# Attention with both heads of a pair side by side, the V projection spread over it, and the row sums through GpSimd's queue

## What is computed

```
h = layernorm(x) * (1 + ca) + sa                  # sa, ca, ga, ... from silu(c) @ wmod
q, k, v = h @ Wq.T + bq, h @ Wk.T + bk, h @ Wv.T + bv
sim = q @ k.T + bias[bucket(i - j)] * 64**-0.5    # causal mask, no scale on q @ k.T
x = x + ga * (softmax(sim) @ v @ Wo.T + bo)
h = layernorm(x) * (1 + cb) + sb
x = x + gb * (quantize(h) @ ternary(w).T + bias)
```

## Time and profile before

| | us |
|---|---|
| median of 2 runs | 1539.74 (1536.56 to 1542.92) |
| the profiled execution | 1533.55 |
| its slowest core, first to last instruction (core 4) | 1531.6 |
| the other cores | 1494.5 to 1517.7 |
| TensorE matmul busy, core 4 | 1048.7 (68%) |
| VectorE, ScalarE, GpSimd busy | 588.8, 435.2, 119.8 |

### The profile page before, as it was taken

The page is one execution under the profiler, slowest core; times in us unless marked ns, Lnnn a source line. Parts: engine busy times, 40 slices in busy tenths (PEclk is TensorE's granted clock), DMA queues, the critical chain, the costliest instruction groups (busy, mean ns, idle before and its releaser), DMA issues.

```text
span 1531.6 us, 17931 instructions; the slowest of 8 cores (1494.5 to 1531.6 us)
## 1 busy us (share of the span) xinstructions
PE 1048.7 (68%) x3933; PEld 364.3 (24%) x3933; DVE 588.8 (38%) x1412; ACT 435.2 (28%) x784; POOL 119.8 (8%) x230
## 2 busy tenths in 40 slices
PE   0344521499998999989989989989879910011168
PEld 0000200142422422422423423324213300000033
DVE  0061751222412522422323223224325628666667
ACT  0001310045155155154253352451640010222200
POOL 0111221011010110110110110000000000000000
PEclk9555555675855855855756757657858955555579
DMA  8665113410010010110100100000000000000013
GB/s 276 219 220 170 15 15 57 76 13 9 6 11 7 9 12 4 11 12 2 13 10 3 14 8 1 1 2 1 2 2 1 1 28 0 0 0 0 1 69 151
DMA packets 44669, 55.65 MB, mean 36 GB/s; under 512 B 32909, under 2 KB 36317, under 8 KB 41480
## 3 DMA queue, kind: packets, MB, share of 16 engines
q0 software_dynamic: 32352, 33.59, 10.6%
q1 hardware_dynamic: 12216, 20.93, 4.1%
HBM read 52.68 MB, written 10.20 MB: 41 GB/s over the span
## 4 chain that ended last, share of the span: by engine, by line
PE 64%; DVE 16%; DMA 11%; issue 5%; ACT 3%; SPq 1%; DVEq 1%; ACTq 0%; POOLq 0%
PE p_oacc L690 19%; PE p_s L659 17%; PE p_s L615 8%; PE p_s L633 5%; DMA swm<-wm 4%; PE p_s L745 4%; PE p_f L877 4%; DMA sx<-x 2%; PE p_s L585 2%; DMA srowb<-dtaus 2%; DVE shT L416 2%; PE p_mod L374 2%; DVE soT L717 2%; PE p_s L637 1%; DVE stmp L841 1%
## 5 line engine op out<-in xcount | busy, mean ns | idle before, releaser
L669 ACT ACTIVATE sPt<-p_s 128x512 bf16<-128x512 f32 (+3 forms) x640 | 320.7, 535 | 534.0 <-DVE sv L641 281.9
L690 PE MATMUL p_oacc<-sPt,sv 128*65 128x512 bf16 (+3 forms) x640 | 317.1, 550 | 31.1 <-DVE sPt L676 26.0
L659 PE MATMUL p_s<-sqt,skt 64*128 64x512 bf16 (+3 forms) x640 | 301.8, 521 | 8.9 <-DVE soT L591 7.1
L865 PE MATMUL p_tr<-sid,sy 128*128 128x128 bf16 x128 | 25.6, 271 | 203.9 <-DVE sy L861 187.0
L682 DVE TENSOR_TENSOR sPt<-sPt,sE 128x112 bf16<-128x112 bf16 x48 | 10.4, 217 | 339.9 <-ACT sPt L669 339.9
L690 PEld LDWEIGHTS p_oacc<-sPt,sv 128*65 128x65 bf16 x640 | 81.5, 134 | 236.5 <-issue 227.8
L659 PEld LDWEIGHTS p_s<-sqt,skt 64*128 64x128 bf16 x640 | 63.8, 106 | 220.4 <-issue 217.5
L676 DVE TENSOR_TENSOR sPt<-sPt,sE 128x240 bf16<-128x240 bf16 (+1 forms) x256 | 66.0, 268 | 112.3 <-ACT sPt L669 111.7
L633 PE MATMUL p_s<-swv,shT 128*128 128x128 bf16 x1024 | 79.2, 220 | 0.4 <-DVE sv L641 0.4
L374 PE MATMUL p_mod<-swm,scsil 128*1 128x512 f32 x96 | 44.4, 618 | 50.4 <-DMA swm<-wm 49.8
L615 PE MATMUL p_s<-shT,swq 128*128 128x512 bf16 x256 | 72.3, 448 | 7.9 <-DVE sqt L622 5.3
(11 more groups left out here) (104 smaller groups left out, 849.2 us busy)
## 6 DMA issues: line engine op xcount, KB each, us to landing
swm<-wm POOLq DMA_DIRECT2D x24, 1024.0 KB, 5.6
sx<-x SPq DMA_DIRECT2D x16, 512.0 KB
out<-sx SPq DMA_DIRECT2D x16, 512.0 KB
swq<-wq POOLq DMA_DIRECT2D x64, 32.0 KB, 2.1
swk<-wk POOLq DMA_DIRECT2D x64, 32.0 KB, 2.1
swv<-wv POOLq DMA_DIRECT2D x64, 32.0 KB, 2.1
swo<-wo POOLq DMA_DIRECT2D x8, 256.0 KB, 4.0
dtau<-srep SPq DMA_DIRECT2D x16, 96.0 KB
```

Of the source, the lines that this page charges most:

```text
L659: o=o, qc=qc: e.matmul(pb[:, qoff:512], skt[o:o + 64, 128 * kt:128 * (kt + 1)], sqt[o:o + 64, 512 * qc + qoff:512 * (qc + 1)], start=True, ...
L669: sq.add("scalar", lambda e, kt=kt, qoff=qoff, pb=pb: e.activation(sPt[:, kt % 4, qoff:512], pb[:, qoff:512], AF.Exp, bias=EXPB, scale=F1) ...
L690: qc=qc, nkt=nkt: e.matmul(p_oacc[:, 512 * qc + qoff:512 * (qc + 1)], sv[:, kt, 65 * hb:65 * hb + 65], sPt[:, kt % 4, qoff:512], start=(kt ...
L865: sq.add("tensor", lambda e, b=b, c=c, pp=pp: e.transpose(p_tr3[pp][:], sy3[:, b, 128 * c:128 * (c + 1)], sid128[:]), reads=[f"sy:{b}", "s ...
```

## The change

- The two heads of a pair are worked side by side. For each key tile there are two Q K matmuls, one for each half of the array's rows, two exps, two P V matmuls. Q K runs one tile ahead, and `sPt` has two slots for each head.
- `p_oacc` is replaced by two banks, `p_o2[0]` and `p_o2[1]`, used again in every query chunk. The copies to `soT` and of the row sums therefore stand at the end of each chunk.
- The V projection of the next pair is spread in 17 steps (a memset, then 16 groups) over the 40 key-tile steps of this pair's attention, in banks of its own (`p_v`), and `sv` is doubled. The first pair's V projection stays ahead of the attention.
- The row sums are stored in bfloat16, two rows for a pair. `epi_A` reads them back with a load from GpSimd's queue that makes float32 of them; it is written behind chunk 0 of the next pair. `epi_B` has one load that repeats the reciprocals over 64 rows, in place of the four matmuls; it is written behind chunk 1 for head 0 and behind chunk 2 for head 1.

The diff, cut to its core:

```diff
-            sv = sb2("sv", [128, NT, 130], BF16)
-            sPt = sb2("sPt", [128, 4, 512], BF16)
+            sv = sb2("sv", [128, 2, NT, 130], BF16)
+            sPt = sb2("sPt", [128, 2, 2, 512], BF16)
             sE = sb2("sE", [128, NH, 240], BF16)
-            srows1 = sb2("srows1", [1, 4, 512], F32)
-            srs16 = sb2("srs16", [16, 128], F32)
-            srs16b = sb2("srs16b", [16, 128], BF16)
-            srecb4 = sb2("srecb4", [1, 2048], BF16)
-            p_oacc = ps2("p_oacc", [65, SEQ])
+            srowsb = [sb2(f"srowsb{i}", [1, 4, 512], BF16) for i in range(2)]
+            srs32 = sb2("srs32", [32, 128], F32)
+            srs32b = sb2("srs32b", [32, 128], BF16)
+            srbt = sb2("srbt", [128, 2048], BF16)
             p_s = [ps2(f"p_s{i}", [128, 512]) for i in range(4)]
-            sv4 = sv[:].rearrange("p t (g c) -> p t g c", c=65)
+            p_o2 = [ps2(f"p_o2{i}", [65, 512]) for i in range(2)]
+            p_v = [ps2(f"p_v{i}", [128, 128]) for i in range(2)]
+            sv4 = sv[:].rearrange("p b t (g c) -> p b t g c", c=65)
 
...
+                sq.add("gpsimd", lambda e: e.dma_start(
+                    out=srs32[:],
+                    in_=dsumB2[:].rearrange("h (p j) -> (h p) j", p=16)),
+                    reads=["dsB2"], writes=["srs32"], dma=True)
+                sq.add("vector", lambda e: e.reciprocal(srs32[:], srs32[:]),
+                       reads=["srs32"], writes=["srs32"])
+                sq.add("vector", lambda e: e.tensor_copy(srs32b[:], srs32[:]),
+                       reads=["srs32"], writes=["srs32b"])
                 sq.add("sync", lambda e: e.dma_start(
-                    out=srs16[:],
-                    in_=dsum[:].rearrange("o (p j) -> (o p) j", p=16)),
-                    reads=["dsum"], writes=["srs16"], dma=True)
-                sq.add("vector", lambda e: e.reciprocal(srs16[:], srs16[:]),
-                       reads=["srs16"], writes=["srs16"])
-                sq.add("vector", lambda e: e.tensor_copy(srs16b[:], srs16[:]),
-                       reads=["srs16"], writes=["srs16b"])
-                sq.add("sync", lambda e: e.dma_start(
-                    out=dsumb[:].rearrange("o (p j) -> (o p) j", p=16),
-                    in_=srs16b[:]),
-                    reads=["srs16b"], writes=["dsumb"], dma=True)
-                sq.add("sync", lambda e: e.dma_start(
-                    out=srecb4[:], in_=dsumb[:]),
-                    reads=["dsumb"], writes=["srecb4"], dma=True)
-
-            def epi_B(d0, o0):
+                    out=dsumB3[:].rearrange("h (p j) -> (h p) j", p=16),
+                    in_=srs32b[:]),
+                    reads=["srs32b"], writes=["dsB3"], dma=True)
+
+            def epi_B(d0, hb0):
+                o0 = 64 * hb0
+                src = AP(dsumB3, 2048 * hb0, [[0, 64], [1, 2048]])
+                sq.add("sync", lambda e, src=src, o=o0: e.dma_start(
+                    out=srbt[o:o + 64, :], in_=src),
+                    reads=["dsB3"], writes=[f"srbt:{hb0}"], dma=True)
                 for qc in range(NQC):
-                    pb = p_s[qc % 4]
-                    pt = f"ps:{qc % 4}"
-                    sq.add("tensor", lambda e, qc=qc, pb=pb: e.matmul(
-                        pb[0:64, :], ones1[:, 0:64],
-                        srecb4[0:1, 512 * qc:512 * (qc + 1)],
-                        start=True, stop=True),
-                        reads=["srecb4"], writes=[pt])
-                    sq.add("vector", lambda e, qc=qc, o=o0, d=d0, pb=pb,
-                           pt=pt: e.tensor_mul(
+                    sq.add("vector", lambda e, qc=qc, o=o0, d=d0: e.tensor_mul(
                         soT[o:o + 64, d, 512 * qc:512 * (qc + 1)],
                         soT[o:o + 64, d, 512 * qc:512 * (qc + 1)],
-                        pb[0:64, :]),
-                        reads=[pt, "soT"], writes=["soT"])
-
-            epi = {"a": None, "b": None}
+                        srbt[o:o + 64, 512 * qc:512 * (qc + 1)]),
+                        reads=[f"srbt:{hb0}", "soT"], writes=["soT"])
 
...
+            def vproj_steps(d):
...
+                def memset_ones(vb=vb):
+                    sq.add("vector", lambda e, vb=vb: e.memset(
+                        sv4[:, vb, :, :, 64:65], 1.0),
+                        writes=[f"svones:{vb}"])
+                steps.append(memset_ones)
                 for t in range(NT):
+                    def grp(t=t, wb=wb, vb=vb, d=d):
+                        pv = p_v[t % 2]
+                        pvt = f"pv:{t % 2}"
+                        for c in range(NCH):
+                            sq.add("tensor", lambda e, wb=wb, c=c, t=t,
+                                   pv=pv: e.matmul(
+                                pv[:],
+                                shT[:, c, 128 * t:128 * (t + 1)],
+                                swv[:, wb, c, :], start=(c == 0), stop=False),
+                                reads=[f"wv:{wb}", f"hT:{c}:{t // 4}"],
+                                writes=[pvt])
+                        sq.add("tensor", lambda e, d=d, pv=pv: e.matmul(
+                            pv[:], ones1[:],
+                            sbvb[:, 128 * d:128 * (d + 1)],
+                            start=False, stop=True),
+                            reads=["bvb", "ones1"], writes=[pvt])
+                        sq.add("vector", lambda e, t=t, vb=vb, pv=pv: e.tensor_copy(
+                            sv4[:, vb, t, :, 0:64],
+                            pv[:].rearrange("p (g c) -> p g c", c=64)),
+                            reads=[pvt], writes=[f"sv:{vb}:{t}"])
...
+            prev = None
+            for d in range(NP):
+                vb = d % 2
+                qkproj(d)
+                if d == 0:
+                    for st in vproj_steps(0):
+                        st()
                 if d + 2 < NP:
                     wload(d + 2)
+                vsteps = vproj_steps(d + 1) if d + 1 < NP else []
+                vinj = [0]
+                step_idx = [0]
+                TOT = sum(4 * qc + 4 for qc in range(NQC))
...
+                    def emit_pv(hb, kt, qc=qc, nkt=nkt, vb=vb):
+                        qoff = max(0, 128 * kt - 512 * qc)
+                        sl = kt % 2
+                        sq.add("tensor", lambda e, kt=kt, qoff=qoff, hb=hb,
+                               sl=sl, nkt=nkt, vb=vb: e.matmul(
+                                   p_o2[hb][:, qoff:512],
+                                   sv[:, vb, kt, 65 * hb:65 * hb + 65],
+                                   sPt[:, sl, hb, qoff:512],
+                                   start=(kt == 0), stop=(kt == nkt - 1)),
+                               reads=[f"pt:{sl}:{hb}", f"sv:{vb}:{kt}",
+                                      f"svones:{vb}"],
+                               writes=[f"po:{hb}"])
+
+                    emit_qk(0, 0)
+                    emit_qk(1, 0)
+                    for kt in range(nkt):
+                        if kt + 1 < nkt:
+                            emit_qk(0, kt + 1)
+                            emit_qk(1, kt + 1)
+                        for hb in (0, 1):
+                            emit_sm(hb, kt)
+                            emit_pv(hb, kt)
+                        step_idx[0] += 1
+                        if vsteps:
+                            want = (step_idx[0] * len(vsteps)) // TOT
+                            while vinj[0] < want:
+                                vsteps[vinj[0]]()
+                                vinj[0] += 1
+
+                    if prev is not None:
+                        if qc == 0:
                             epi_A()
+                        elif qc == 1:
+                            epi_B(prev, 0)
+                        elif qc == 2:
+                            epi_B(prev, 1)
+
+                    for hb in (0, 1):
+                        sq.add("vector", lambda e, qc=qc, hb=hb, d=d: e.tensor_copy(
+                            soT[64 * hb:64 * hb + 64, d,
+                                512 * qc:512 * (qc + 1)],
+                            p_o2[hb][0:64, :]),
+                            reads=[f"po:{hb}"], writes=["soT"])
+                        sq.add("scalar", lambda e, qc=qc, hb=hb: e.activation(
+                            srowsb[hb][0:1, qc, :], p_o2[hb][64:65, :],
                             AF.Identity, bias=F0, scale=F1),
+                            reads=[f"po:{hb}"], writes=[f"srb:{hb}"])
+
+                while vsteps and vinj[0] < len(vsteps):
+                    vsteps[vinj[0]]()
+                    vinj[0] += 1
+                for hb in (0, 1):
+                    sq.add("sync", lambda e, hb=hb: e.dma_start(
+                        out=dsumB2[hb:hb + 1, :],
+                        in_=srowsb[hb][:].rearrange("o q j -> o (q j)")),
+                        reads=[f"srb:{hb}"], writes=["dsB2"], dma=True)
+                prev = d
+
+            epi_A()
+            epi_B(prev, 0)
+            epi_B(prev, 1)
```

(33 more changed lines are left out.)

123 lines of the change are left out of this document (41 added, 82 removed).

## The result

The changed kernel takes 1571.5 us (median of 11 runs, 1568.0 to 1579.7), and the kernel before 1537.8 beside it (10 runs). The ratio is 1.0273, 95% interval 1.0236 to 1.0309: slower by 2.7%. The forecast was 1586.0. Medians here are over all runs and ratios over the undisturbed ones alone, since in some runs the cores of one die show a lower clock and take longer. The profiled execution took 1574.5, its slowest core (core 5) spanned 1572.8.

The account below looks back on a forecast made before the run. TensorE's own order and clock were taken to set the pace. Pairs of 91, five times 130.6, 79.5 and 69.5 make 893 against 847.1, 46 more: 1579.5 profiled, plus 6.2 for the median, 1586 us; range 1535 to 1680.

Parts of the forecast that it names:

- The stop: Pairs two to six, after chunk 0: TensorE idles 51 us each, as the row-sum load stands behind 24 weight loads.
- the chain from first to last: GpSimd's 24 weight loads of a pair, one after another: 59.6 us to the last load.
- Steps: One key tile for both heads in attention: 1.63 us at the low clock, 1.04 at the high clock.
- V group: One of 16 V projection groups among the attention steps: adds 0.68 us at the high clock, 1.1 at the low.
- The clock: Chunks 1 to 3: rises in chunk 1, drops at some ends; a quarter from high (51 us) to low (72).
- Chunk ends: Next P V waits for copies, exps for row-sum copies: 2.0 us over the steady pace high, 1.0 low.
- the tail: Chunks 1 to 3 of a pair, after chunk 0 and any stall: 57 us, or 47 in the last pair.
- the end: From the last pair's attention to the output projection: stays about as long as the 15.6 us before.
- That the stop doesn't come: Rival, pairs two to six, chunk 0: no wait on GpSimd's queue, 80.5 us a pair, 1336 in all; chance 0.05.
- Q K one after the other: Rival, attention steps: the two Q K run serially, low step 1.96 us, 10 more a pair, 1666; chance 0.13.
- Clock low throughout: Rival, all attention: chunks 1 to 3 take 72 us instead of 57, 115 more in all, 1701; chance 0.08.
- Clock high: Rival, attention after the first tiles: clock stays high, 49 us less in all, 1537; chance 0.10.

Follow-up runs that it names:

- an earlier place: Changed kernel with GpSimd's load of the row sums issued ahead of the weight loads on the same queue: 1317.9 us, ratio 0.858.
- loads that don't wait: Changed kernel with a tag for each weight slice, so weight loads no longer wait for each other to land: 1339.5 us, ratio 0.872.
- the queue alone: Kernel before the change with one word changed, its row sums loaded by GpSimd instead of SP: 1794.5 us, ratio 1.170.
- unpaired run: Against the version with SP, the two Q K of a step no longer adjacent (Q K, P V per head in turn): 1625.3 us, ratio 1.061.
- version with SP: Changed kernel with the row sums, still bf16, loaded by SP's queue instead of GpSimd's: 1322.8 us, ratio 0.861.
- copies-first run: Against the version with SP, the copies out of `p_o2` written ahead of `epi_A` and `epi_B` at chunk ends: 1271.8 us, ratio 0.830.
- the lead over the ends: Against the copies-first run, next chunk's first Q K and exps ahead of the copies, V groups at an end behind them: 1270.0 us, ratio 0.829.

## Why the prediction was right

*The stop.* Forecast: idle for 51 us, TensorE going on at 73.6 into the pair. Measured in the second pair: 52.9, and 455.93 - 382.80 = 73.1. The parts held, with small misses that cancel: GpSimd's first load is issued 7.6 into the pair, forecast 9.2; the chain from first to last, forecast 59.6, took 60.7 (390.39 to 451.07); from there to the next P V it is 4.9, forecast 4.8. The stop begins at 20.2 (402.99), forecast 22.5. The experiments show the mechanism from four sides, and leave no other cause for the stop (another queue, an earlier place, loads that don't wait, the queue alone).

*Steps.* The disputed price was the distance between the two Q K of a step, 0.10 to 0.43 us. Measured at the low and then the high clock (core 5):

```profile
494.24 1.06 PE L636 MATMUL p_v<-swv,shT 128*128 128x128 bf16 x8
...
495.45 0.61 PE L677 MATMUL p_s<-sqt,skt 64*128 64x512 bf16 x2
495.99 1.06 PE L716 MATMUL p_o<-sPt,sv 128*65 128x512 bf16 x2
496.98 0.61 PE L677 MATMUL p_s<-sqt,skt 64*128 64x512 bf16 x2
```
```profile
350.15 0.39 PE L677 MATMUL p_s<-sqt,skt 64*128 64x512 bf16 x2
...
351.02 0.39 PE L677 MATMUL p_s<-sqt,skt 64*128 64x512 bf16 x2
...
352.77 0.39 PE L677 MATMUL p_s<-sqt,skt 64*128 64x512 bf16 x2
```

Two Q K take 0.61 together, no longer than one alone (0.60). The ends of matmuls are modelled in a profile, but the starts say the same: in most pairs the second Q K starts 3 or 4 ns after the first, and the P V behind them starts 0.54 us after the two, where it starts 0.53 after a single one in the unpaired run (low clock). The step is 496.98 - 495.45 = 1.53, where I had 1.63; the 0.10 isn't there. So the Trainium skill's rule (TensorEngine Tiling (Array Packing), Key Properties: tiles run in parallel) holds in this trace, and the 1.55 that I had worked out by it was nearer than my own figure. At the high clock a step without a V group takes 1.04 (from 1149.86 to 1150.90, last pair), as forecast; two steps and a V group take 352.77 - 350.15 = 2.62, forecast 2 x 1.04 + 0.68 = 2.76. A V group at the low clock takes 495.45 - 494.24 = 1.21, forecast 1.1. The summary of the profile agrees, though it mixes the two clocks: the groups of Q K fall from 301.8 us to 124.2, over 640 instructions.

*The clock.* I put it a quarter of the way to low. From the resumption at 455.9 to 513.7 the pair takes 57.8, forecast 57. It does rise in chunk 1 and drop at chunk ends, 0.84 over the stretch. In the first pair it was high nearly throughout (0.96 over the pair), so chunks 1 to 3 took 49 (382.80 - 333.70) instead of 57; with chunk 0 a little shorter as well, the pair took 82 where I had 91. This is the largest miss among the terms. I gave two reasons for the clock. The first, Q K in pairs, is borne out by the unpaired run: without the pairs it stays low. The second, the V groups, isn't seen on the version with SP (0.84 with and without them), and is seen only once the ends are short (0.91 against 0.83).

*Chunk ends.* The sum had 2.0 over the steady pace, from ScalarE alone. It missed that in chunks 1 and 2 the copies stand behind four multiplies of `epi_B`: 2.9 to 3.05 us of waiting, plus the low stretch. The forecast for the tail came out right because this error and the steps' went opposite ways, which was luck. The copies-first run measures it: 49 us over the whole kernel, which the forecast's terms don't contain.

*The sum.* Pairs: 82.0 + 130.9 + 129.8 + 128.4 + 128.6 + 129.8 + 78.6 + 67.2 = 875.3, and with the 17.4 at the end 892.7. I had 893 for the pairs alone, and 15.6 for the end (in the chain of waits the DMA into `srbt` takes 3.9 us of it now). So the pairs came to 17.7 less, 9 of it in the first; the end took 1.8 more, the part behind it 379.3 against 377.5, and this core reached its first pair at 300.8, where core 4 had at 291.4. That is 1579.5 - 17.7 + 1.8 + 1.8 + 9.4 = 1574.8, against 1574.5 profiled. The rest of the 14.5 by which 1586.0 was too high is the median, 3 under the profiled execution now, where I had carried over 6.2 above it. That the whole is within 1% is partly luck too: the 17.7 by which the pairs were too dear are half hidden by the 9.4 of a core that starts later. In either kernel the cores reach their first pair between 291 and 302 us, and the slowest core was an early one before and a late one after.

*The rivals.* That the stop doesn't come: refuted as to this kernel, but its time, 1336, is what the version with SP comes to (1322.8). Q K one after the other: refuted by the 0.61. Clock low throughout: refuted, 0.72 to 0.75 over pairs that stand still for 52 us, and 0.84 from the resumption on. Clock high: 0.84 in the tail, between the two. What was to show the forecast wrong (a wait under 40 us, Q K 0.43 apart, a clock below 0.7 in chunks 2 and 3, where it is 0.89 from 476.0 to 513.7) didn't occur. The times of two rivals don't follow from their own terms: a pair without the stall is 22.5 + 57 = 79.5, not 80.5, and a low clock throughout adds 7 x 15 + 7 = 112, not 115; neither changes a verdict.

## What to carry to other kernels

Before an instruction is moved to another queue, list what stands ahead of it there and whether those entries wait for each other: here a load of 16 KB behind 24 serial ones turned a gain of 14% into a loss of 2.7%, and the same load issued ahead of them mends it. In an engine's own queue, write what frees a buffer (1.5 us of copies) ahead of what merely has to be done some time (the multiplies, the reciprocal): this was worth another 49 us. Two matmuls of half the rows belong next to each other, in halves of their own; the version with SP and the copies first, 1272 us or 17% under the kernel before, beats both kernels, and none of the others tried beats it (the lead over the ends, 1270, is the same within what can be told).

## What was unexpected of the hardware

Two matmuls of 64 rows in different halves, next to each other in the queue, cost what one costs (0.61 for both, 0.60 for one, low clock; the second starts 3 or 4 ns after the first). The order of those two instructions decides the clock of the whole attention: next to each other, it comes back to 1.00 within 7 us of a chunk's end even at 1.53 a step; apart, with TensorE busy for 90.9 of 102.5 us, more than in the attention of any pair of the paired order, it stays at 0.52. In the kernel before, too, it was low at 33.7 busy us of 33.7. Between the two runs two things differ, which rows work at the same time and how often TensorE changes between 64 and 128 rows, and no run here tells which of them counts. And a stop of only 3 us at a chunk's end was followed by some 6 us at the low clock; without V groups at the ends, waits of 1.25 and 1.35 us were followed by a fall too, and with them waits of 0.68 and 0.75 were not.
